# Upper triangle for the middle attention of a four-layer graph network, and score rows that go through DRAM

## The reference, cut to what matters

```python
# layer 0: two normed products with adj and its transpose, batch norm over all graphs
# layer 1: Wh = h @ W.T;  e = leaky(s[i] + t[j], 0.2);  softmax over the neighbours j;  alpha @ Wh
# layer 2: (adj holds 0 or 1, so of its four kinds of edges only the first is used)
e = einsum('bid,bjd,dk->bkij', h, h, A);  e = leaky_relu(e, 0.2)
scores = where(adj == 1, e[:, 0], -9e15)
out = softmax(scores) @ h
# layer 3: as layer 1 with a W and an a of its own, then elu
```

## Time and profile before

| | |
|---|---|
| median of 3 runs | 1597.4 us (1595.6 to 1599.42) |
| profiled execution | 1601.0 us, its span 1599.2 us |
| TensorE clock, mean over the span | 0.958 of full speed |
| layer 0's two stages | to about 440 us |
| first gram (graph 0) starts | 514.2 us |
| inner turns | 65.7 us each |
| last weighing | starts at 1556.8 us |

### The profile page before, as it was taken

The page is one execution under the profiler, slowest core; times in us unless marked ns, Lnnn a source line. Parts: engine busy times, 40 slices in busy tenths (PEclk is TensorE's granted clock), DMA queues, the critical chain, the costliest instruction groups (busy, mean ns, idle before and its releaser), DMA issues. The chain is left out here.

```text
span 1599.2 us, 32655 instructions
## 1 busy us (share of the span) xinstructions
PE 1469.1 (92%) x12740; PEld 1271.3 (79%) x12740; DVE 1135.3 (71%) x3197; ACT 921.6 (58%) x1825; POOL 207.6 (13%) x209
## 2 busy tenths in 40 slices
PE   5899998899746979999999999999999999999984
PEld 5899998555334859889898898988989889898774
DVE  4666564787645577887888888878787787886653
ACT  4677775122124765766757666566675766755620
POOL 6343430000000001011010111110111101010000
PEclk9999998899957989999999999999999999999996
DMA  9999991466711222213223132231322313212010
GB/s 207 226 204 207 197 204 65 144 232 243 276 45 43 71 64 57 79 41 106 74 60 93 28 113 73 54 93 28 113 75 52 97 36 102 66 34 62 27 34 27
DMA packets 109598, 161.94 MB, mean 101 GB/s; under 512 B 9472, under 2 KB 61312, under 8 KB 107392
## 3 DMA queue, kind: packets, MB, share of 16 engines
q1 hardware_dynamic: 85248, 117.86, 24.7%
q0 software_dynamic: 19584, 33.56, 11.4%
q10 hardware_dynamic: 4608, 8.39, 1.5%
HBM read 151.40 MB, written 41.94 MB: 121 GB/s over the span
## 5 line engine op out<-in xcount | busy, mean ns | idle before, releaser
L1343 PE MATMUL ps<-hV,wts_B 128*128 128x129 f32 x2048 | 246.2, 276 | 3.2 <-ACT wts_B L1142 3.0
L1343 PE MATMUL ps<-hP_A,wts_A 128*128 128x129 f32 x2048 | 239.2, 277 | 6.1 <-DVE wts_A L898 3.3
L1343 PE MATMUL ps<-hP_C,wts_C 128*128 128x129 f32 x2048 | 239.1, 277 | 5.9 <-DVE wts_C L898 5.9
L1343 PEld LDWEIGHTS ps<-hV,wts_B 128*128 128x128 f32 x2048 | 238.2, 192 | 4.6 <-ACT wts_B L1142 4.3
L1343 PEld LDWEIGHTS ps<-hP_A,wts_A 128*128 128x128 f32 x2048 | 234.5, 193 | 8.5 <-DVE wts_A L898 5.1
L1343 PEld LDWEIGHTS ps<-hP_C,wts_C 128*128 128x128 f32 x2048 | 234.4, 193 | 8.2 <-DVE wts_C L898 5.6
L903 DVE SCALAR_TENSOR_TENSOR wts_B<-wts_B 128x1024 f32<-128x1024 f32 x128 | 153.9, 1221 | 29.8 <-ACT wts_B L1138 29.8
L898 DVE SCALAR_TENSOR_TENSOR wts_A<-row_A,least_A,ring_A 128x1024 f32<-128x1024 f32 x128 | 161.2, 1275 | 9.1 <-ACT row_A L1122 8.3
L293 ACT ACTIVATE maskT<-ps 128x1024 fp8e4<-128x1024 bf16 x128 | 131.3, 1026 | 56.7 <-PE ps L335 45.3
L1138 ACT COPY wts_B<-ps 128x1024 f32<-128x1024 f32 x128 | 129.5, 1012 | 59.8 <-PE ps L1330 59.8
L898 DVE SCALAR_TENSOR_TENSOR wts_C<-row_C,least_C,ring_C 128x1024 f32<-128x1024 f32 x128 | 162.3, 1274 | 0.8 <-DMA ring_C<-maskT_scratch 0.6
(11 more groups left out here) (229 smaller groups left out, 2551.6 us busy)
## 6 DMA issues: line engine op xcount, KB each, us to landing
adj_b<-in_adj POOLq DMA_DIRECT2D x120, 256.0 KB, 9.8
maskT_scratch<-maskT SPq DMA_DIRECT2D x16, 1024.0 KB, 6.8
ring_A<-maskT_scratch SPq DMA_DIRECT2D x64, 256.0 KB, 3.2
off<-maskT_scratch SPq DMA_DIRECT2D x32, 512.0 KB, 6.6
ring_C<-maskT_scratch SPq DMA_DIRECT2D x64, 256.0 KB, 3.1
xa<-in_x SPq DMA_DIRECT2D x16, 512.0 KB, 4.2
whT_scratch<-whT_s ACTq DMA_DIRECT2D x32, 256.0 KB, 6.9
whT_b<-whT_scratch SPq DMA_DIRECT2D x16, 512.0 KB, 4.7
```

The costliest lines, as they stand in the source:

```text
L1343: last = nc.tensor.matmul(Q_SLOTS[c // 2 % 2][:, c % 2, 0:PW], wts[x][:, j, c * P:c * P + P], src[:, j, :], start=(j == 0), stop=(j == T - 1))
```

## The change

1. The gram computes for row tile j only the columns from j*128 on, with three products; `pen_id` and `complement` go. `keep_scores`, `leaky` and `score_exps` work on these columns.
2. `turn_rows` on TensorE transposes the exponentials above the diagonal into PSUM, in five groups behind the first five tiles of stage A. `lower` on VectorE multiplies them by the mask into the lower triangle of `wts_B`; `upper` on GpSimd multiplies the upper one in place. The weighing of B waits for both.
3. `rows` is one transpose, `row_power` a pass of 8 x 128 with a 4 KB store on ScalarE's queue; `load_row` on SP loads the row into all partitions (512 KB).
4. Orders: C's `turn_h` stands ahead of gram 0, its values behind gram 1 in one piece; A's first weights come after C's `moments`, two instead of one are left to the next turn's start; the ELU's passes move to the middle of stage A and behind B's last `shares`; `quotient_exps` goes behind all `score_exps`. The last turn with a gram (i == B) has a list of its own, in which C's first four tiles come ahead of B's weighing and the other four behind it.

```diff
@@ SP
                     def load_off(b, h):
                         if b > 0:
-                            sp.wait_ge(S["B", "gram"], (b - 1) * T + 4 * h + 4)
+                            sp.wait_ge(S["B", "up"], b * T)
+                            sp.wait_ge(S["B", "low"], b * LT)
...
+                    def load_row(x, b):
+                        sp.wait_ge(S[x, "s_out"], (b + 1) * 16)
+                        if b > 0:
+                            sp.wait_ge(S[x, "wts"], b * T)
+                        sp.dma_start(row_e[x][:, :], row_dram[x][b % 2].rearrange("t p -> (t p)").partition_broadcast(P)) \
+                            .then_inc(S[x, "s_row"], 16)
@@ GpSimd
+                    def upper(b, k):
+                        if k % 4 == 0:
+                            pool.wait_ge(S["B", "ring"][k // 4], (b + 1) * 16)
+                        if k < LT:
+                            pool.wait_ge(S["B", "turned"], b * LT + k + 1)
+                        else:
+                            pool.wait_ge(S["B", "exps"], b * T + k + 1)
+                        w = wts["B"][:, k, k * P:N]
+                        pool.tensor_tensor(w, w, off_fp8[:, k, k * P:N], ALU.mult).then_inc(S["B", "up"], 1)
...
+                        if i >= 1:
+                            upper(i - 1, 0)
+                            upper(i - 1, 1)
                         if i + 1 < B:
                             rstd("A", i + 1)
+                        if i >= 1:
+                            for k in range(2, T):
+                                upper(i - 1, k)
@@ VectorE
+                    def lower(b, k):
+                        dve.wait_ge(S["B", "turned"], b * LT + k + 1)
...
+                        nc.vector.tensor_tensor(wts["B"][:, k + 1:T, ks], turned(k).rearrange("p (t q) -> p t q", q=P),
+                                                off_fp8[:, k + 1:T, ks], ALU.mult).then_inc(S["B", "low"], 1)
@@ VectorE, run(i), stage A: what stands between tiles 5 and 7, as it is after
+                            shares("A", i, 2)
                             add("A", i, 0, newB, oldB)
                             shifts("A", i + 1)
+                            lower(i - 1, 5)
+                            lower(i - 1, 6)
+                            elu_positive()
                             weights("C", i - 2, 1)
                             weights("C", i - 2, 2)
                             shares("A", i, 3)
@@ VectorE, run(i), behind B's last shares, as it is after
                             shares("B", i - 1, 3)
+                            elu_negative()
                             highest_share("B", 1)
                             add("B", i - 1, 1, newC, oldC)
                             stats("C", newC, 0)
                             shares("C", i - 2, 0)
                             stats("C", newC, 1)
                             moments("C")
+                            weights("A", i + 1, 0)
+                            lowest("A")
+                            shifts("C", i - 1)
+                            weights("A", i + 1, 1)
                             shares("C", i - 2, 1)
                             split_g(i)
                             split_ag(i)
+                            weights("A", i + 1, 2)
+                            weights("A", i + 1, 3)
                             shares("C", i - 2, 2)
+                            weights("A", i + 1, 4)
                             weights("A", i + 1, 5)
@@ ScalarE
+                    def row_power(x, b):
+                        act.wait_ge(S[x, "s_made"], b + 1)
+                        if b > 0:
+                            act.wait_ge(S[x, "s_out"], b * 16)
+                        nc.scalar.activation(row_s[x][:, :], LAST[x][0:T, 0:P], ACT.Exp, scale=1.0 - SLOPE).then_inc(S[x, "s_kept"], 1)
+                        act.wait_ge(S[x, "s_kept"], b + 1)
+                        if b > 1:
+                            act.wait_ge(S[x, "s_row"], (b - 1) * 16)
+                        act.dma_start(row_dram[x][b % 2], row_s[x][:, :]).then_inc(S[x, "s_out"], 16)
@@ ScalarE, run(i), gram stage, as it is after
                             relu_hT("C", i - 2, "A", min(i + 1, B))
                             keep_scores(i - 1, 0)
                             keep_scores(i - 1, 1)
                             score_exps(i - 1, 0)
                             keep_scores(i - 1, 2)
                             exps("C", i - 2)
                             keep_scores(i - 1, 3)
                             keep_scores(i - 1, 4)
                             row_power("C", i - 2)
                             keep_scores(i - 1, 5)
...
                             keep_scores(i - 1, 7)
                             score_exps for j = 1 to 7, then quotient_exps(i - 3)
@@ TensorE
-                        for c in range(CH):
-                            cs = slice(c * HALF, (c + 1) * HALF)
+                        for c in range(j * P // HALF, CH):
+                            cs = slice(max(c * HALF, j * P), (c + 1) * HALF)
...
-                            last = nc.tensor.matmul(P_SLOTS[j % 2][:, cs], pen_id[:, :], off_fp8[:, j, cs], start=False, stop=True)
+                    def rows(x, b, free):
+                        take(free, 1, S[x, "s_kept"], b + 1)
+                        pe.wait_ge(S[x, "us"], b + 1)
+                        nc.tensor.transpose(LAST[x][0:T, 0:P], us[x][:, :], ident[:, :]).then_inc(S[x, "s_made"], 1)
+            GROUPS_T = ((0, 1), (1, 2), (2, 3), (3, 5), (5, 7))
+            TURNED = [(1, 0), (0, 0), (1, 0), (0, 0), (0, HALF), (1, 0), (1, HALF)]
+                    def turn_rows(b, k0, k1):
+                        take(free_p, TURNED[k0][0], S["B", "low"], b * LT + k1)
+                        for k in range(k0, k1):
+                            pe.wait_ge(S["B", "exps"], b * T + k + 1)
+                            for t in range(k + 1, T):
+                                last = nc.tensor.transpose(turned(k)[:, (t - k - 1) * P:(t - k) * P], wts["B"][:, k, t * P:t * P + P],
+                                                           ident[:, :])
+                            last.then_inc(S["B", "turned"], 1)
@@ TensorE, weigh
+                            if c == 0 and x == "B":
+                                pe.wait_ge(S["B", "up"], b * T + j + 1)
+                                pe.wait_ge(S["B", "low"], b * LT + min(j, LT))
```

More of the change, by code:

```diff
@@ L750, in gnn_stack_kernel @@
             S["C", "quo_exp"] = csem("C_quo_exp")
-            for n in ("var", "rstd", "shift", "h", "hT_made", "ahi", "lo", "off", "gram", "kept", "lrelu", "exps", "tile", "rec", "quo", "done"):
+            for n in ("var", "rstd", "shift", "h", "hT_made", "ahi", "lo", "gram", "kept", "lrelu", "exps", "turned", "low", "up", "tile", "rec", "quo", "done"):
                 S["B", n] = csem(f"B_{n}")
@@ L943, in run, with elu_positive, elu_negative @@
                         newA = xA[(i + 1) % 2]
+                        def elu_positive():
+                            dve.wait_ge(S["C", "quo"], (i - 2) * PARTS)
+                            nc.vector.scalar_tensor_tensor(old[:, :, :], quo[:, :, :], 0.0, old[:, :, :], ALU.max, ALU.add)
+                        def elu_negative():
+                            dve.drain()
+                            dve.wait_ge(S["C", "quo_exp"], i - 2)
+                            nc.vector.scalar_tensor_tensor(old[:, :, :], elu[:, :, :], 1.0, old[:, :, :], ALU.min,
+                                                           ALU.add).then_inc(S["C", "done"], 1)
                         if post:
@@ L948, in run @@
                         if AA:
+                            weights("A", i, 6)
                             weights("A", i, 7)
@@ L977, in run @@
                             leaky(i - 1, 7)
+                        if i == B:
+                            elu_positive()
+                            lower(i - 1, 0)
+                            weights("C", i - 2, 0)
+                            weights("C", i - 2, 1)
+                            lower(i - 1, 1)
+                            weights("C", i - 2, 2)
+                            lower(i - 1, 2)
+                            weights("C", i - 2, 3)
+                            lower(i - 1, 3)
+                            lower(i - 1, 4)
+                            elu_negative()
+                            weights("C", i - 2, 4)
+                            lower(i - 1, 5)
+                            lower(i - 1, 6)
+                            for j in range(5, T):
+                                weights("C", i - 2, j)
+                            shares("C", i - 2, 0)
+                            shares("C", i - 2, 1)
+                            shares("B", i - 1, 0)
+                            shares("B", i - 1, 1)
+                            add("B", i - 1, 0, newC, oldC)
+                            dve.drain()
+                            stats("C", newC, 0)
```

(12 more changed lines are left out.)

208 lines of the change are left out of this document (103 added, 105 removed).

## The result

The changed kernel takes 1611.0 us (median of 4 runs, 1609.5 to 1611.7) against 1596.5 for the kernel before in the same call: a ratio of 1.0081, interval [1.0062, 1.0099]. It is slower by 0.8%, where I had forecast 0.6% faster. The profiled spans are 1609.9 and 1599.2 us, 10.7 apart.

A forecast was written before the change was run, and what follows sets the result against it. TensorE, 92% busy, was taken to bound the kernel. Turns -16, head -4 and tail +11 summed to -9 us: 1592 against the profiled 1601.0, 1588 as the median of runs; range for 8 in 10, 1555 to 1622.

The forecast's parts named there:

- 13 x -1.2 = -16: 13 full turns (stages C, gram, A, B) of the pipeline over graphs, each 1.2 us shorter: 16 us less.
- TensorE's own work: Its four stages: 59.3 us a turn instead of 65.7; 84 us less over 13 turns if TensorE stayed the bound.
- Stage C, 2.4 us stall: Ahead of layer 3's turning: VectorE's third reciprocal starts 14.7 us after B's fourth, so TensorE waits 2.4 us.
- Stage B, 0.8 us stall, and 0.7 for the port: TensorE waits 0.8 us for layer 1's maximum; GpSimd holding VectorE adds 0.7 us a turn.
- Undisturbed turn, 64.5: One full turn: 63.8 us without GpSimd plus 0.7 for the port, 1.2 less than before.
- GpSimd at 2.3 ns a column: GpSimd's upper products over 4608 columns: 10.8 us a turn, the last ending 28.4 us after the gram's start.
- rival 2: GpSimd ends last and delays B's first tile: at 3.3 ns a column turn 67.5 us, 1628 us; chance 0.2.
- Rival 3: VectorE and GpSimd exclude each other at full price, 2.5 us a turn: turn 66.3, 1612 us; chance 0.1.
- Rows hidden inside a turn: Score rows through DRAM: 7.4 us needed, about 9 available for layer 1, so hidden with 1.6 us to spare.
- Head -4: Start of the kernel: later first weights, but no complements and two shorter gram stages, together 4 us less.
- Tail +11: End: last turn's gram, B and C 57 us against 52.8, the last graph's norm 1.5 and row 4.5 later.
- Rival 1: TensorE keeps the pace because VectorE's lags overlap: turn 60.6 us, 1537 us, half way 1565; chance 0.17.

The follow-up runs named there:

- e9: All of the change but the triangle (whole gram kept), with VectorE's order much as in e7 and a later result store: 1579.0 us, 0.9884 of the kernel before.
- e1: Changed kernel with layer 3's third reciprocal moved ahead of layer 1's weights passes 2 and 3 in stage C: 1599.9 us, 1.0008 of the kernel before.
- e2: Changed kernel with the ELU's first pass behind the leaky passes and its second ahead of B's last reciprocal: 1595.2 us, 0.9982 of the kernel before.
- e5: Changed kernel with 20 unread transposes put into TensorE's stall ahead of layer 3's turning: 1607.4 us, 1.0054 of the kernel before.
- e4: Changed kernel with GpSimd's upper products over 8 columns each, leaving out most of layer 2's upper mask: 1592.8 us, 0.9957 of the kernel before.
- e7: Changed kernel with a new order of VectorE's reciprocals, weights, leaky and ELU passes, and no special last-turn list: 1575.1 us, 0.9847 of the kernel before.
- e11: e10 with GpSimd's power put back behind its second product, ahead of the third: 1571.4 us, 0.9828 of the kernel before.
- e8: e7 with layer 1's residual among the leaky passes, the first ELU pass later, GpSimd's third product ahead of its power: 1604.9 us, 1.0041 of the kernel before.
- e6: Kernel before with the score rows through DRAM as the only change: 1625.4 us, 1.0175 of the kernel before.
- e12: e10 with layer 1's score columns read ahead of layer 2's shifts and layer 3's ahead of the seventh weights pass: 1550.6 us, 0.9694 of the kernel before.
- e10: e7 with the first ELU pass ahead of A's third reciprocal and GpSimd's third product ahead of its power: 1557.6 us, 0.9739 of the kernel before.
- e3: Changed kernel without the special lists of the last turn with a gram, on VectorE, ScalarE and TensorE: 1601.0 us, 1.0028 of the kernel before.

## Why the prediction was wrong

It failed in its term **13 x -1.2 = -16**, which measured +3.6, and in a part of the pipeline it left out. Two things were wrong in the term: the 2.4 us stall was taken at its length, without the falls of the clock behind it (10 us over the 13 turns), and an undisturbed turn takes 65.2 us where I had 64.5 (9 us).

- *TensorE's own work* (59.3 us a turn): 65.2 less 4.9 of waits is 60.3, 1.0 more; 0.6 of it in the gram stage (9.3 instead of 8.7) and 0.3 in B (17.45; where it has no wait, in e9, it takes the 17.2 I gave it).
- *Stage C, 2.4 us stall*: right in place, cause and size (2.37; 14.77 us between the reciprocals against 14.7; the shift's wait 1.45). e1 takes it away by moving the third reciprocal ahead of two weights passes. Of the parts of my sum the ELU's pass, 1.3, was not needed for it: e2 has it elsewhere and the stretch is 14.77 us still.
- *What the stall does beyond its length*: missed, the largest part of the error. I took every stall at face value. Behind this one the clock was down in six of thirteen turns, 1.3 to 1.5 us each, 8.5 together, and once behind B's (20.95 instead of 19.09). That is the 10 us by which the 13 turns exceed 13 x 65.2. Filling the stall gives back 7.1 of them (e5), taking it away some 8 (e1).
- *Gram stage, 10.0*: 10.15, with the waits at gram 5 and 7 (0.19 and 0.47) and 0.20 for the maximum; 0.9 of waits, not 1.3.
- *Stage B, 0.8 us stall, and 0.7 for the port*: together 1.5, measured 1.64 at the maximum and B 1.9 over the 17.2 I gave TensorE's work there. The split was wrong: with the ELU moved (e2) the wait is 0.50, and without most of the products (e4) 0.53. Each alone takes away 1.1 of the 1.64, more than my 0.8 and 0.7, so the two overlap.
- *Undisturbed turn, 64.5*: 65.2. Short by 0.7: TensorE's own work 1.0 more, the waits 0.3 less (4.9 against 5.2). This and the clock turned -16 into +3.6.
- *GpSimd at 2.3 ns a column*: 2.0 where nothing holds it (2.02 us for 1024), and with the held ones 12.0 us a turn instead of 10.8. It never ended last: rival 2 falls in the changed kernel. In e7 and e11, where B comes nearer, it does (0.66 to 1.3 us a turn).
- *The other direction of the port*, which no row showed: it exists. The weights pass at 1056.39 took 2.10 us. Rival 3's mechanism is thus right, its price in a steady turn was 1.1 us (e4) and not 2.5, since VectorE had idle time behind. The Trainium skill (SBUF — State Buffer, "Who interferes with whom") has it as an exclusive lock for the whole instruction; e8's pass, issued at 1047.51 and ended 0.55 us behind the product, agrees. Which of the two was issued first did not decide it alone: in e7 the product, issued while a leaky pass ran, also let the ELU's pass by, which was issued 0.66 us later and took its usual 1.22 (3.75 us for the product instead of 2.02).
- *Rows hidden inside a turn*: right. No weights pass waits for a row there; the 12.3 us of such waits in the page lie at the ends. e6 shows that this holds only because the first weights were moved back.
- *Head -4*: -10.0. I had counted two gram stages without following the two half-filled turns: by TensorE's positions the first weighing of A comes 2.3 us earlier, the two gram stages are 2.3 and 6.4 shorter (7.3 in a steady turn), the A stages in all 1.5 longer, the B stage 0.5 shorter. Some of it is chance: in e1 to e5 the third graph's A starts between 582.8 and 588.7 us.
- *Tail +11*: +12.6, near in sum and wrong in its parts. I forecast 57 us for the last turn's gram, B and C; it takes 63.5. Its weights passes stand inside GpSimd's products, which I priced in steady turns alone (3.7 us by e4), and behind its waits TensorE's clock falls (granted 0.50, then 0.71). At the very end the last graph's first weighing waits 6.4 us against 2.4: 4.0 for the row, near the 4.5.
- *Left out*: the turn whose A stage has no next graph. Its transposes and B's wait come (+4.4 us) before any gram has paid for them.

Where the expected gain of 84 us went: TensorE's work in a turn fell by 5.4 us (65.7 to 60.3), not 6.4, and 4.9 came back as waits, most of them behind VectorE, which had 12 us idle; the clock's falls took 10 more over the 13 turns. Rival 1, that the idle time would carry it, was right about the capacity and wrong about the order given: e12 takes 3.1 us off the changed kernel's turn with the same instructions. By parts, rows through DRAM with the moved work bring 19 us (e9 to before); the triangle adds 21 in e10 and 28 in e12, 4 in e7, and costs 26 in e8 (each against e9, whose order was not tuned further; these are differences of medians of different calls, good to some 2 us). How far the rest of e12's turn, and its gram-to-C stretch at the tail (58 us against 53 before), could be shortened wasn't tried.

## What to carry to other kernels

When work comes off the bounding engine, list what each remaining stage waits for last and re-order the next engine's queue for it; a queue with 20% idle time can still be late at every place that counts. Put the step that frees the next stage (a reciprocal, a maximum) ahead of bulk passes that nobody wants yet, and look for where it lands next: moved alone, the lag moved with it. Bulk passes with two SBUF operands on VectorE should not stand beside GpSimd's products; products and passes that read PSUM can.

## What the runs showed of the hardware

- A stall of 2.4 us on TensorE was followed by a granted clock at the lower level in six of thirteen turns, same program, same wait. Filled with transposes nobody reads, none of twelve fell. Over the changed kernel, e2, e3 and e4, which all have this stall, it was 20 of 52 turns. B's waits of 1.64 us left the clock alone; of its eight waits of 1.95 to 1.99 us in the changed kernel, e1, e3 and e5, three were followed by a fall; and one turn in each of four runs had 2.72 us in C, with a fall in e2 alone. What decides which turns fall isn't settled.
- In the changed kernel a fall cost 1.3 to 1.5 us where TensorE sets the pace (the gram stage; 1.9 the one time in B), and nothing in e8's stage A, where the next stage waits for VectorE in any case.
- GpSimd and VectorE hold each other in both directions: a leaky pass 2.22 us instead of 0.68, a product 3.75 instead of 2.02. A pass that reads PSUM and one tile of SBUF is not held (1.08 us beside a product in e8, 1.08 in the changed kernel).
- A 4 KB store and the 512 KB broadcast load behind it: the load is issued 1.2 us after the store was, so my 2.2 for the store was high.
